# Windowed attention and a ternary feed-forward layer on one core: softmax sums divided after the value products, work moved to GpSimd, and stage C one slot later

## What is computed

```python
x = x + attn(layernorm(x))      # 16 heads of 16, causal window of 64 keys, softmax, Wo
x = x + ffn(layernorm(x))       # relu(x W1q^T + b1) W2q^T + b2, W1q and W2q ternary, width 1024
...
scores = einsum('bhqd,bhkd->bhqk', q, k) * scale + bias
attn = softmax(scores)          # exp(s - max) / sum
out = einsum('bhqk,bhkd->bhqd', attn, v)
```

## Time and profile before

| what | value |
|---|---|
| runs | 691.65, 692.78, 693.37 us, median 692.78 |
| profiled execution, first to last instruction (its span) | 690.4 us |
| profiled execution, own time | no figure beside the span; the median of the runs is 2.4 us more than the span |
| TensorE busy | 649.0 us, 94% |
| VectorE busy | 628.3 us, 91% |
| ScalarE busy | 623.9 us, 90% |
| GpSimd busy | 618.0 us, 90% |
| DMAs of SyncE's queue | 51.2% of 16 DMA engines' span |

### The profile page before, as it was taken

One profiled execution on the slowest core, in us unless ns is written; L12 is line 12 of the kernel. 1 busy time (PEld: TensorE's weight loads), 2 busy tenths in 40 slices (PEclk: granted clock), 3 DMA queues, 4 the chain that ended last, 5 costly groups with the idle time before them and its releaser, 6 DMA issues.

```text
span 690.4 us, 24485 instructions
## 1 busy us (share of the span) xinstructions
PE 649.0 (94%) x8048; PEld 552.7 (80%) x8048; DVE 628.3 (91%) x1596; ACT 623.9 (90%) x2649; POOL 618.0 (90%) x869
## 2 busy tenths in 40 slices
PE   7668699999999999999999999999999999998887
PEld 5446488888888888888888888887888888887776
DVE  5779889999999999999999999999999999899864
ACT  5689899999999999999999999998999999898833
POOL 7388999999999999999999999999899999999930
PEclk9879989999999999999999999999999999999999
DMA  8576656465756656475756657475665646464000
GB/s 293 80 98 103 75 96 73 77 86 74 125 73 99 98 99 95 77 95 72 128 68 101 96 92 105 51 117 74 102 91 99 74 82 71 61 93 70 18 31 31
DMA packets 497988, 61.17 MB, mean 89 GB/s; under 512 B 470724, under 2 KB 493510, under 8 KB 497864
## 3 DMA queue, kind: packets, MB, share of 16 engines
q1 hardware_dynamic: 487160, 50.82, 51.2%
q10 hardware_dynamic: 10704, 8.80, 4.2%
HBM read 11.86 MB, written 8.39 MB: 29 GB/s over the span
## 4 chain that ended last, share of the span: by engine, by line
PE 40%; POOL 32%; issue 10%; ACT 9%; DVE 6%; DMA 1%; SPq 0%; POOLq 0%; DVEq 0%; ACTq 0%
POOL p L393 13%; POOL tl L417 10%; PE ps L1089 9%; PE ps L1077 7%; ACT p L496 6%; PE ps L987 5%; POOL th L411 5%; PE ps L967 5%; PE ps L1024 4%; PE ps L1035 3%; PE ps L1050 3%; ACT hTh L573 1%; PE ps L1062 1%; POOL rstdC L386 1%; PE ps L960 1%
## 5 line engine op out<-in xcount | busy, mean ns | idle before, releaser
L496 ACT ACTIVATE p<-ps,negm 128x96 f32<-128x96 f32 x1024 | 340.3, 375 | 8.4 <-DVE negm L711 7.7
L417 POOL TENSOR_TENSOR tl<-pt,th 128x384 f16<-128x384 f32 x256 | 234.6, 916 | 16.3 <-ACT th L505 1.8
L496 ACT ACTIVATION_READ_ACCUMULATOR p<-ps,negm 128x1 f32 x1024 | 248.5, 244 | 0.0
L393 POOL TENSOR_TENSOR p<-p,rden 128x384 f32<-128x384 f32 x256 | 214.3, 837 | 7.3 <-DVE rden L718 6.9
L724 DVE STREAM_TRANSPOSE pt<-p 128x384 f32<-128x384 f32 x256 | 141.5, 553 | 14.3 <-POOL p L393 12.9
L711 DVE TENSOR_REDUCE negm<-ps 128x4 f32<-128x384 f32 x256 | 136.0, 531 | 10.4 <-PE ps L967 8.1
L967 PE MATMUL ps<-k,qbd 128*128 128x96 f16 x1536 | 125.2, 208 | 0.0
L967 PEld LDWEIGHTS ps<-k,qbd 128*128 128x128 f16 x1536 | 106.0, 99 | 9.6
L987 PE MATMUL ps<-th,vb 128*128 128x96 f16 (+1 forms) x1120 | 97.1, 202 | 1.8 <-POOL tl L417 1.8
L1077 PE MATMUL ps<-xTCh,w1T 128*128 128x256 f16 x512 | 97.6, 272 | 0.8 <-ACT xTCh L568 0.8
L573 ACT ACTIVATE hTh<-ps 128x512 f16<-128x512 f32 x128 | 79.6, 623 | 19.9 <-PE ps L1077 19.7
(11 more groups left out here) (139 smaller groups left out, 1486.7 us busy)
## 6 DMA issues: line engine op xcount, KB each, us to landing
k<-kst SPq DMA_DIRECT2D x32, 288.0 KB, 4.1
vb<-vd SPq DMA_DIRECT2D x256, 32.0 KB, 2.6
out<-x SPq DMA_DIRECT2D x32, 256.0 KB, 2.5
qbd<-qs SPq DMA_DIRECT2D x254, 32.0 KB, 2.3
x<-in_L_attn_hidden ACTq DMA_DIRECT2D x15, 512.0 KB, 5.4
kw<-kst SPq DMA_DIRECT2D x31, 192.0 KB, 3.8
k<-kst SPq DMA_DIRECT2D x31, 144.0 KB, 3.4
vb<-in_L_ffn_W SPq DMA_DIRECT2D x2, 1024.0 KB, 7.6
```

Source lines behind the costliest of these rows:

```text
L393: e.tensor_tensor(p3, p3, rden[n % 4][:, :].unsqueeze(2).to_broadcast([128, 4, 96]), ALU.mult).then_inc(s_nm, 1)
L417: e.tensor_tensor(tl[g % 2][:, o], pt[n % 3][:, :], th[g % 2][:, o], ALU.subtract).then_inc(s_lo, 1)
L496: ins = e.activation(p[:, 96 * u:96 * u + 96], bank[:, 96 * u:96 * u + 96], ACT.Exp, bias=m[:, u:u + 1], accum_out=r[:, u:u + 1])
```

## The change

What it does, in words:

- `norm` (the multiplication of the 256 x 384 exponentials) and the 256 reciprocals are gone. `turn` follows the exponentials directly, so transposition, `low` and `values` come one slot earlier (`L_TURN` 2, `L_PART` 3, `PV_LAG` 8).
- The sums of 8 rows (a pair of groups, half the heads of a chunk, t = 0 or 1) are collected in `rsum[t]`. VectorE takes one reciprocal and transposes it (`inverse`, `turn_inverse`, lag 9), SyncE writes it to DRAM (`park_r`, lag 10) and reads it back spread over 16 partitions per head (`widen_r`, two DMAs of 128 KB, lag 12), and GpSimd multiplies `osum` by it (`o_norm`, lag 13). GpSimd then splits `osum` for both halves (`o_split`, lag 14).
- All 16 `th` roundings of a chunk are GpSimd's (`ROUNDED` and ScalarE's `high` are gone). GpSimd also does the rows of the second norm (`c_norm`), and ScalarE no longer does.
- `A_V` goes from (8, 12) to (10, 13): both halves of V later. Stage C is one slot later (`C_WO`, `C_T`, `C_F`, `C_Y`, `OUT_DMA`, `X_DMA`).
- The bias tile `bt` is no tile of its own any more, but lies in `hT` until the weights are ready, so its clear, copy and subtraction are two instructions each, and ScalarE's `magnitudes` waits for them once.

```diff
-A_T, A_Q, A_K, A_V = (1, 2), (6, 14), (6, 15), (8, 12)
+A_T, A_Q, A_K, A_V = (1, 2), (6, 14), (6, 15), (10, 13)
...
-C_WO, C_STATS, C_RSTD, C_NORM = (7, 10), (8, 13), (10, 15), (10, 15)
-C_T, C_F, C_Y = (11, 16), (13, 19), (18, 24)
-OUT_DMA, X_DMA = (26, 26), 33
+C_WO, C_STATS, C_RSTD = (8, 11), (9, 13), (11, 15)
+C_T, C_F, C_Y = (12, 17), (14, 20), (19, 25)
+OUT_DMA, X_DMA = (27, 27), 34
...
-PV_LAG, O_ADD, O_SPLIT0, O_SPLIT1 = 9, 10, 17, 10
-ROUNDED = (0, 1, 4, 5, 7, 9, 10, 12, 13, 14, 15)
-L_MAX, L_EXP, L_INV, L_NORM, L_TURN, L_PART = 0, 1, 2, 2, 3, 4
+PV_LAG, O_ADD, O_SPLIT = 8, 9, 14
+R_INV, R_PARK, R_WIDEN, R_MUL = 9, 10, 12, 13
+L_MAX, L_EXP, L_TURN, L_PART = 0, 1, 2, 3
...
+def pair_at(n, lag):
+    h, r = divmod(n - lag, 8)
+    return divmod(h, 2) if r == 0 and 0 <= h < 2 * NCH else None
...
+            def park_r(c, t):
+                e.wait_ge(s_rt, 2 * c + t + 1)
+                if c >= 1:
+                    e.wait_ge(d_r[t], 32 * c)
+                e.dma_start(parked[t], rturn[t][:, :]).then_inc(d_p[t], 16)
+
+            def widen_r(c, t):
+                e.wait_ge(d_p[t], 16 * (c + 1))
+                if c >= 1:
+                    e.wait_ge(s_on, 2 * (c - 1) + t + 1)
+                for g in range(2):
+                    e.dma_start(rwide[t][64 * g:64 * g + 64, :],
+                                bass.AP(tensor=parked[t].tensor, offset=512 * g, ap=[[1024, 4], [0, 16], [1, 512]])
+                                ).then_inc(d_r[t], 16)
...
-            def norm(n):
...
-            def o_split(c):
-                e.wait_ge(s_osum, 4 * c + 2)
+            def o_norm(c, t):
+                e.wait_ge(d_r[t], 32 * (c + 1))
+                e.wait_ge(s_osum, 4 * c + 2 * t + 2)
+                e.tensor_tensor(osum[:, t, :], osum[:, t, :], rwide[t][:, :], ALU.mult).then_inc(s_on, 1)
+
+            def o_split(c, t):
+                e.wait_ge(s_on, 2 * c + t + 1)
                 if c >= 1:
                     e.wait_ge(s_c, USE[c - 1, "wo1"] + 1)
...
+                e.tensor_copy(oT[0][:, t, :], osum[:, t, :]).then_inc(s_oh, 1)
+                e.wait_ge(s_oh, 2 * c + t + 1)
+                e.tensor_tensor(oT[1][:, t, :], osum[:, t, :], oT[0][:, t, :], ALU.subtract).then_inc(s_ol, 1)
...
                 if 0 <= n - L_PART < NQ:
                     low(n - L_PART)
-                if 0 <= n - L_NORM < NQ:
-                    norm(n - L_NORM)
-                gg = group_at(n, O_SPLIT0)
-                if gg is not None and gg % 4 == 1:
-                    o_split(gg // 4)
+                ct = pair_at(n, R_MUL)
+                if ct is not None:
+                    o_norm(*ct)
+                ct = pair_at(n, O_SPLIT)
+                if ct is not None:
+                    o_split(*ct)
...
-            def inverse(n):
+            def inverse(c, t):
+                e.wait_ge(s_ex, 16 * c + 8 * t + 8)
+                e.reciprocal(rden[t][:, :], rsum[t][:, :, :, :].rearrange("p g i u -> p (g i u)")).then_inc(s_rd, 1)
+
+            def turn_inverse(c, t):
...
-            def o_low(c):
...
                 e.wait_ge(s_td, 8)
-                e.wait_ge(s_olo0, c + 1)
-                e.wait_ge(s_olo1, c + 1)
+                e.wait_ge(s_ol, 2 * c + 2)
```

More of the change, by code:

```diff
@@ L41 @@
 SLOTS = range(-44, NQ + 48)
-def rounded(n):
-    return n // 16 * (16 - len(ROUNDED)) + sum(q not in ROUNDED for q in range(n % 16 + 1))
 def chunk_at(n, pos, first):
@@ L178, in build @@
         negm = [sb(f"negm{i}", [128, 4], f32) for i in range(4)]
-        rsum = [sb(f"rsum{i}", [128, 4], f32) for i in range(4)]
-        rden = [sb(f"rden{i}", [128, 4], f32) for i in range(4)]
+        rsum = [sb(f"rsum{t}", [128, 2, 4, 4], f32) for t in range(2)]
+        rden = [sb(f"rden{t}", [128, 32], f32) for t in range(2)]
+        rturn = [sb(f"rturn{t}", [128, 32], f32) for t in range(2)]
+        rwide = [sb(f"rwide{t}", [128, CH], f32) for t in range(2)]
         th = [sb(f"th{i}", [128, 1600], f16) for i in range(2)]
@@ L191, in build @@
         nthr = sb("nthr", [128, 2], f32)
+        parked = [nc.dram_tensor(f"parked{t}", (128, 32), f32, kind="Internal").ap() for t in range(2)]
         banks = [ctx.enter_context(nc.psum_tensor(f"ps{i}", [128, 512], f32)) for i in range(8)]
@@ L435, in _ @@
                         rstd_c(2 * c + h)
+                        c_norm(c, h)
                 c = norm_at(n, A_RSTD, N_RSTD)
@@ L515, in a_norm @@
                 ins.then_inc(s_xnA, 1 if c else 2)
-            def c_norm(c, u):
-                h = 2 * c + u
-                e.wait_ge(s_rsC, h + 1)
-                if h >= 1:
-                    e.wait_ge(s_c, USE[(h - 1) // 2, f"t{(h - 1) % 2}"] + 1)
-                for t in range(2):
-                    ins = e.activation(xnC[:, t, 0:D - 1], xs[c % NX][:, 2 * u + t, 0:D - 1], ACT.Identity,
-                                       bias=shiftC[u][:, t:t + 1], scale=rstdC[u][:, t:t + 1])
-                ins.then_inc(s_xnC, 1)
-            def o_high(c):
-                e.wait_ge(s_osum, 4 * c + 4)
-                if c >= 1:
-                    e.wait_ge(s_c, USE[c - 1, "wo1"] + 1)
-                e.activation(oT[0][:, 1, :], osum[:, 1, :], ACT.Copy).then_inc(s_ohi, 1)
             def a_t(c, k):
@@ L639, in _ @@
                         a_norm(c, u)
-                gg = group_at(n, O_SPLIT1)
-                if gg is not None and gg % 4 == 3:
-                    o_high(gg // 4)
         @block.vector
```

112 lines of the change are left out of this document (54 added, 58 removed).

## The result

The changed kernel takes **873.38 us** (median of 4 runs, 867.63 to 876.86), the kernel before 692.21 (4 runs on the same chip). The ratio is 1.261, 95% interval 1.256 to 1.266. The prediction was 830 us with a range of 768 to 872: slower as forecast, by the mechanism forecast, and a little beyond the range's end. The step of the forecast that failed is the size of its term 3, the read-back behind q1: 5.8 us a pass were forecast, 8.36 measured.

What follows compares the result with a forecast made beforehand. The prediction took a loop through SyncE's queue, nearly as long as TensorE's work, as the bound. Span 690.4 + 6.5 + 129 (14 passes x 9.2) + 2.5 = 828, plus 2.4 to the median: 830 us, range 768 to 872.

Steps and rivals of the forecast that it cites:

- term 3: On SyncE's queue the read-back stands behind q1; value products behind slot 8 start 5.8 us behind q1's end.
- last V product to V's first DMA: First part of the loop through SyncE, from TensorE's product to the queue: taken as 2.55 us.
- term 2: On SyncE's queue, the write of the reciprocals between V and the keys adds one issue, 0.45 us.
- term 4: From the value products to the last V product: 14.2 us, and 0.45 us more because Wo needs the split.
- term 5: TensorE idle around slot 8 lets the granted clock fall: 2.5 us lost per pass, bounds 0 and 3.4.
- term 6: Before the repeated passes, from the first chunk on: V comes later and the chain of term 3 adds, +6.5 us.
- term 7: From slot 8 of the last chunk: GpSimd starts later, with o_norm and splits before Wo, +2.5 us, between 0 and 6.
- Term 1: V and stage C a slot later: 3.2 us of TensorE's work moves behind slot 8, giving 14.5 us to the last V product.
- only q1 is late: Rival: the read-back is no later than q1's landing or GpSimd runs behind; pass 41.7 us, some 730 us; chance 0.10.
- This kernel already runs on a loop through SyncE: Kernel before: last V product, V issued, q1 issued and landed, slot 8, next V product; 38.1 us per pass.
- two loops of nearly the same length hide each other: Kernel before: SyncE's loop sums to 38.1 us and TensorE needs nearly all of 39.1, so both must be costed.

Runs made afterwards that it cites:

- r_act: The changed kernel with the write and read-back of the reciprocals issued from ScalarE's queue instead of SyncE's, at the same lags; 779.82 us.
- r_first: The changed kernel with the read-back issued one slot earlier from the same queue, ahead of q1's transfers; 817.04 us, ratio 1.176.
- no_read: The changed kernel without write and read-back, multiplying by ones (output undivided), V and stage C placed as in the kernel before; 701.47 us, ratio 1.010.
- land8: The changed kernel with each read-back cut into 8 transfers of 16 partitions instead of 2 of 64; 893.84 us.
- before_v_late: The kernel before with V's products alone moved later, from (8, 12) to (10, 13); 757.93 us, ratio 1.095.
- v_early: The changed kernel with V's products alone back at (8, 12), reciprocals still on SyncE's queue; 866.4 us.
- fill: The changed kernel with 28 idle matmuls on TensorE before the wait for the first value products of each chunk but the first; 881.91 us, ratio 1.271.
- before_c_late: The kernel before with all of stage C alone one slot later; 735.37 us, ratio 1.060.
- before_vsplit: The kernel before with V's 16 transfers split, 8 where they were and 8 behind q1's; 692.84 us, ratio 0.998.

## Why the prediction missed by 43 us

The mechanism was right in its place and its order: SyncE's queue, the read-back behind q1, GpSimd standing still, TensorE before the value products behind slot 8. The multiplication of the second half waits 5 us or more in each of 15 chunks, as forecast (164.8 us in all), and r_act, r_first and no_read show it as the cause. The other 51 us of the 215.8 stand before the first half's multiplication; the forecast had no wait of GpSimd there. The sizes, term by term:

| step | forecast | measured |
|---|---|---|
| last V product to V's first DMA | 2.55 | 4.07 |
| V's first DMA to q1's end, with the write (term 2) | 22.85 | 22.17 |
| q1's end to the value products (term 3) | 5.8 | 8.36 |
| value products to the next V (term 4), with the clock (term 5) | 17.15 | 16.14 |
| pass | 48.4 | 50.75 |
| value products at slot 8 of the second chunk (term 6) | 92.4 | 97.8 |
| from the last such point to the end (term 7) | 59.0 | 62.4 |

The span is 97.8 + 14 x 50.4 + 62.4 = 865.8, where the forecast had 92.4 + 14 x 48.4 + 59.0 = 829. The mean of 14 passes between these points is 50.4. The 37 us are 28 from the passes, 5.4 from the first chunks and 3.4 from the end. Of the remaining 6, 5 stand between span and median (7.6 us here, where the profiled execution was the fastest of the four, and 2.4 before), and 1 is the forecast's rounding.

One row of the page of the kernel before bears on term 3, and the forecast didn't use it: the keys, on the same queue, with a pattern that also reads rows more than once (size, and us from issue to landing):

```profile
k<-kst SPq DMA_DIRECT2D x32, 288.0 KB, 4.1
```

- **Term 3 was mis-sized, and it is the step that failed.** It came to 8.36 us instead of 5.8, 2.6 us more in each pass and 36 us in 14; the misses of the other terms nearly cancel within the pass. The landing was taken as 2.5 us behind the second issue, 2.1 behind its end, from the store of 256 KB, with the landing of the x load (3.4 us) as the upper bound. It is 4.3 us behind the end of the issue (5.61 - 1.30), 4.9 behind the start of the second. The two issues take 1.30 us instead of 0.95, the multiplication 1.26 instead of 1.16. The nearest rows by size weren't the nearest by pattern: all were transfers of many outer blocks. And the keys' row above had a higher bound than 3.4 us. The Trainium skill, page "DMA: Bandwidth & Descriptors", section "Anatomy of one DMA — SWDGE (gpsimd) path", fits transfers issued by GpSimd; used as an estimate for this one from SyncE's queue, it would give 2.3 us. The trace doesn't agree for this pattern (4.9 us), and comes near it for the other (land8: 1.9 us for 32 KB, estimate 2.1).
- **V product to V's DMA was taken as unchanged, 2.55 us.** It became 4.07. VectorE sets it, in whose order V's low half stands behind other work. The stall isn't needed for most of it: with V's products at their later place and nothing else it is 3.65 (before_v_late), and with the stall but V early 3.07 (v_early). All the way behind the stall was costed on TensorE's rows, 14.65 us plus clock, where VectorE's and ScalarE's backlog ends last (fill). These two errors of opposite kind, a clock that costs nothing behind the stall and a VectorE that costs 1.5 us ahead of the V products and 1.5 behind them, nearly cancel. That is luck.
- **Term 5, the clock.** That it would fall in every pass was right (clock 0.915 for 0.983, and 55 us more of TensorE's busy time). That it costs 2.5 us per pass was not: with the clock kept up behind the stall the time doesn't fall. The Trainium skill, page "TensorE: Matmul & The Clock Gate", section "HAM oscillation — how this bites in real kernels", describes a kernel that waits for a DMA in every tile and starts every tile at the lower clock. The trace agrees for the clock: behind slot 8 it stands at 0.5 for 3.4 to 6.8 us in 11 of the 13 passes of the table. The time that the forecast took it to cost is not there. In before_v_late, where VectorE is busy without a gap for 5.4 us ahead of V's DMA in most passes and not for 12.9, it is (some 1.3 us a pass, the estimate above).
- **Term 1** gave one slot 1.85 us (4.6 us measured in before_v_late, with waits), by leaving out the feed-forward's piece, and took stage C's move as 1.31 us of Wo alone, where before_c_late lost 2.6 us per pass. Behind the stall neither shows, since TensorE isn't what ends last there. Had the read-back been harmless, the forecast of "only q1 is late", 730 us, would have been too low for this reason too; the kernel nearest to that rival, r_act, took 780.
- **"This kernel already runs on a loop through SyncE" was wrong** for the kernel before: before_vsplit takes 6.4 us out of it and gains nothing. The 0.93 us wait in the earlier trace rows was the longest of four such waits in 15 passes, 3.3 us in all. That two loops of nearly the same length hide each other was right, as V's place shows.
- The range's upper end took the landing up to 3.4 us behind the second issue's start. With the keys' 4.1 it would have been 882, and with the measured 4.9 higher still: either holds the result. (Its lower end adds up to 775 from its own terms, not 768.)

## What to carry to other kernels

A transfer put into a queue that is issued in order costs what stands ahead of it, and what stands behind it pays for it. Ask of each new one who waits for it, and what is issued between its data being ready and its own issue: here one slot earlier was worth 56 us and another queue 94. Behind a stall, don't take the way to the next one from the engine that stood still, but from the one that has the most work to make up. And test a bound by making it shorter with nothing else changed, as the split of V's transfers did, before relieving or blaming it.
